# One-hots, selection matrix and centroid parts on 128 rows instead of 120, in a cluster-and-convolve kernel

## The reference

```python
xn = x / jnp.maximum(jnp.linalg.norm(x, axis=1, keepdims=True), EPS)
cn = centroids / jnp.maximum(jnp.linalg.norm(centroids, axis=1, keepdims=True), EPS)
sim = jnp.einsum('bchw,nc->bnhw', xn, cn)
idx = jnp.argmax(sim, axis=1)
onehot = jax.nn.one_hot(idx, N, dtype=x.dtype)                  # N = 40
sum_x = jnp.einsum('bhwn,bchw->bnc', onehot, x)
count = jnp.sum(onehot, axis=(1, 2))
centroids_local = sum_x / jnp.maximum(count, 1.0)[..., None]
gathered = centroids_local[jnp.arange(B)[:, None, None], idx]
delta = jnp.transpose(gathered, (0, 3, 1, 2)) - x
alpha = jnp.exp(-jnp.mean(delta * delta, axis=1, keepdims=True))
y = x + alpha * delta
out = jnp.einsum('oc,bchw->bohw', W, y) + b[None, :, None, None]
return jax.nn.relu(out)
```

## Time and profile before

| | |
|---|---|
| median of the runs | 433.23 us (432.71 to 433.5) |
| profiled execution, its own time | 433.72 us |
| its span, first to last instruction | 431.9 us |
| granted clock of TensorE | 1.000 over the span |
| busy: PE, PEld | 424.5 us (98%), 296.9 us (69%) |
| busy: VectorE, ScalarE, GpSimd | 285.3 us (66%), 243.7 us (56%), 206.8 us (48%) |
| share of PE in the chain that ended last | 95% |

### The profile page before, as it was taken

One profiled execution on the slowest core, in us unless ns is written; L12 is line 12 of the kernel. 1 busy time (PEld: TensorE's weight loads), 2 busy tenths in 40 slices (PEclk: granted clock), 3 DMA queues, 4 the chain that ended last, 5 costly groups with the idle time before them and its releaser, 6 DMA issues.

```text
span 431.9 us, 5788 instructions
## 1 busy us (share of the span) xinstructions
PE 424.5 (98%) x2134; PEld 296.9 (69%) x2134; DVE 285.3 (66%) x377; ACT 243.7 (56%) x329; POOL 206.8 (48%) x102
## 2 busy tenths in 40 slices
PE   8999999999999999999999999999999999999996
PEld 6745466775777667775867757776677758777785
DVE  2458979495775767495873957767674956777730
ACT  5565385566564673564754665656735647555542
POOL 2000565486283582674553862834826745324330
PEclk9999999999999999999999999999999999999999
DMA  8996198976488846859379665878464220222133
GB/s 278 306 289 118 43 250 221 279 217 168 144 232 200 206 186 148 223 142 266 99 194 253 180 160 147 238 193 220 170 152 141 98 99 0 98 99 97 45 112 135
DMA packets 70927, 73.94 MB, mean 171 GB/s; under 512 B 2724, under 2 KB 45732, under 8 KB 70900
## 3 DMA queue, kind: packets, MB, share of 16 engines
q1 hardware_dynamic: 70900, 73.58, 62.0%
HBM read 48.40 MB, written 25.17 MB: 170 GB/s over the span
## 4 chain that ended last, share of the span: by engine, by line
PE 95%; DVE 2%; ACT 1%; issue 1%; POOL 0%; POOLq 0%; DVEq 0%
PE main L793 20%; PE main L795 19%; PE main L794 19%; PE sump L736 10%; PE fa L696 9%; PE gat L767 5%; PE al L774 1%; PE al L815 1%; PE fa L705 1%; PE al L775 1%; PE fa L720 1%; PE main L836 1%; PE al L781 1%; PE gat L781 1%; DVE xt L311 1%; PE gat L808 1%
## 5 line engine op out<-in xcount | busy, mean ns | idle before, releaser
L281 POOL TENSOR_TENSOR z<-z,x 128x1024 f32<-128x1024 f32 x42 | 99.4, 2386 | 148.5 <-DVE z L386 148.5
L793 PE MATMUL main<-yh,wh 128*128 128x512 f32 x376 | 153.1, 407 | 0.0
L795 PE MATMUL main<-yh,wl 128*128 128x512 f32 x376 | 147.1, 391 | 0.0
L794 PE MATMUL main<-yl,wh 128*128 128x512 f32 x376 | 147.0, 391 | 0.0
L288 POOL TENSOR_TENSOR yl<-z,yh 128x1024 fp32r<-128x1024 f32 x44 | 106.1, 2426 | 58.8 <-ACT yh L526 58.8
L366 DVE TENSOR_TENSOR z<-gat,x 128x1024 f32<-128x1024 f32 x46 | 56.2, 1221 | 92.4 <-PE gat L767 92.4
L534 ACT ACTIVATE o<-main,bcol 128x512 f32<-128x512 f32 x96 | 65.9, 687 | 84.5 <-PE main L795 84.4
L793 PEld LDWEIGHTS main<-yh,wh 128*128 128x128 f32 x376 | 70.6, 188 | 20.8 <-issue 4.6
L795 PEld LDWEIGHTS main<-yh,wl 128*128 128x128 f32 x376 | 70.6, 188 | 15.7
L794 PEld LDWEIGHTS main<-yl,wh 128*128 128x128 f32 x376 | 70.7, 188 | 14.5
L526 ACT ACTIVATE yh<-z 128x1024 fp32r<-128x1024 f32 x48 | 50.5, 1052 | 22.9 <-POOL z L281 21.9
(11 more groups left out here) (113 smaller groups left out, 326.9 us busy)
## 6 DMA issues: line engine op xcount, KB each, us to landing
x<-x SPq DMA_DIRECT2D x24, 1024.0 KB, 5.8
out<-o SPq DMA_DIRECT2D x23, 1024.0 KB, 4.9
xs<-x SPq DMA_DIRECT2D x84, 256.0 KB, 6.1
o<-w SPq DMA_DIRECT2D x1, 1024.0 KB, 12.2
out<-o SPq DMA_DIRECT2D x4, 256.0 KB, 2.1
sq<-centroids SPq DMA_DIRECT2D x2, 80.0 KB
bcol<-bias SPq DMA_DIRECT2D x1, 2.0 KB, 11.7
```

Source lines behind the costliest of these rows:

```text
L281: pool.tensor_tensor(z, z, X[g // PARTS % 2][:, pair(h), span(g)], ALU.add).then_inc(y_pool, 1)
L793: t_.matmul(main[:, o % 2, :], WH[:, k, rows], YH[g % 2][:, k, :], start=(k == 0), stop=False)
L794: t_.matmul(main[:, o % 2, :], WH[:, k, rows], YL[g % 2][:, k, :], start=False, stop=False)
L795: last = t_.matmul(main[:, o % 2, :], WL[:, k, rows], YH[g % 2][:, k, :], start=False, stop=(k == KC - 1))
```

## The change

`NK`, the number of columns of `oh3` and `select` and of rows of `ohT`, `part` and `G`, goes from 120 to 128. The last eight columns of `oh3` are set to zero once, at the start on VectorE; those of `select` are zero from the memset on GpSimd that now covers 128 columns. The rows 120 to 127 of `ohT`, `G` and the rest are then computed as zeros. No instruction changes its place in any engine's program; one memset on VectorE is added, and the semaphore `const_done` counts to 8 instead of 7.

```diff
-NK = COPIES * N
+USED = COPIES * N
+
+NK = P
@@
-        oh3 = sb("oh3", [P, PARTS * TILES, COPIES, N], BF16)
+        oh3 = sb("oh3", [P, PARTS * TILES, NK], BF16)
         ohT = [sb(f"oht{j}", [NK, HW], BF16) for j in range(2)]
@@
-        select = sb("select", [P, COPIES, N], F32R)
+        select = sb("select", [P, NK], F32R)
@@
-        select0 = OUT[1][:, 0, 0:NK].rearrange("p (r n) -> p r n", r=COPIES)
+        select0 = OUT[1][:, 0, 0:NK]
+        select_rows = select0[:, 0:USED].rearrange("p (r n) -> p r n", r=COPIES)
@@
-            pool.memset(select0[:, :, :], 0.0).then_inc(ident_done, 1)
+            pool.memset(select0, 0.0).then_inc(ident_done, 1)
@@
-            pool.tensor_copy(select[:, :, :], select0[:, :, :]).then_inc(const_done, 1)
+            pool.tensor_copy(select[:, :], select0).then_inc(const_done, 1)
@@
             v_.memset(oh[:, :, :], 0.0).then_inc(const_done, 1)
+            v_.memset(oh3[:, :, USED:NK], 0.0).then_inc(const_done, 1)
@@
-                a_.activation(oh3[:, :, :, :], oh[:, :, 0:N].unsqueeze(2).to_broadcast(
+                a_.activation(oh3[:, :, 0:USED].rearrange("p s (r n) -> p s r n", r=COPIES), oh[:, :, 0:N].unsqueeze(2).to_broadcast(
                     [P, PARTS * TILES, COPIES, N]), ACT.Copy).then_inc(oh3_done, 1)
@@
-                        last = t_.transpose(dst, oh3[:, slot(u, t), :, :].rearrange("p r n -> p (r n)"), identb[:, :])
+                        last = t_.transpose(dst, oh3[:, slot(u, t), :], identb[:, :])
@@
-                rows = select[:, :, :].rearrange("p r n -> p (r n)")
+                rows = select[:, :]
                 t_.matmul(mean(b), rows, sumsH[:, :], start=True, stop=False)
                 t_.matmul(mean(b), rows, sumsL[:, :], start=False, stop=True).then_inc(cop_done, 1)
```

More of the change, by code:

```diff
@@ L262, in _ @@
                                base=0, pattern=[[-1, P]], channel_multiplier=1).then_inc(ident_done, 1)
-            pool.affine_select(out=select0[:, :, :], in_=select0[:, :, :], compare_op=ALU.not_equal, fill=1.0,
+            pool.affine_select(out=select_rows, in_=select_rows, compare_op=ALU.not_equal, fill=1.0,
                                base=0, pattern=[[0, COPIES], [-1, N]], channel_multiplier=1).then_inc(ident_done, 1)
@@ L425, in _ @@
             v_.reciprocal(s(6), s(5)).then_inc(norm_step, 1)
-            dve.wait_ge(const_done, 7)
+            dve.wait_ge(const_done, 8)
             keep_transposed()
@@ L508, in square @@
                     act.wait_ge(wT_ps, KC)
-                    act.wait_ge(const_done, 7)
+                    act.wait_ge(const_done, 8)
                 elif h == 0:
@@ L850, in _ @@
             transpose_weights(1)
-            pe.wait_ge(const_done, 7)
+            pe.wait_ge(const_done, 8)
             sum_clusters(0, 0)
```

## The result

The change makes the kernel a little faster: 431.33 us (median of 15 runs, 430.95 to 432.24) against 433.14 us for the kernel before (15 runs beside them), a ratio of 0.9964 with a 95% interval of 0.9958 to 0.9971. The medians differ by 1.8 us; the ratio stands for 1.6 us, between 1.3 and 1.8 by its interval. The forecast was no difference.

A forecast was written before the change was run, and what follows sets the result against it. The prediction took TensorE (PE) to bound the kernel. Its terms were all taken as 0, so it forecast the median of the runs before, 433.2 us, no difference (chance 0.84), with a range of 432.3 to 434.2.

The forecast's parts named there:

- the signs: Twelve transposes clearly off 0.83 us, gathers' step reaching 0.23, or a gather's load beginning with the matmul ahead.
- What bounds the kernel: TensorE, busy 424.5 of 431.9 us and 95% of the chain; time changes only where its matmuls follow faster or slower.
- The 96 transposes: One-hots' transposes, 12 per image: loads fall from 133 to about 98 ns, step stays 55 ns; 0 expected.
- the third rival: Faster: the load sets the transposes' step, 3.4 us less, 2.9 for sure, 430.3 us; chance 0.08 with smaller gains.
- The gathers: 96 matmuls with `G` and `ohT` going to 128 rows: step stays 0.22 us; 0 expected, at worst 1.15 us lost.
- the holds: 44 late loads of gathers, 15.8 us idle on PEld; at most about 0.5 us back if full rows end them; 0 taken.
- The second rival: Slower: full rows bring the 96 gathers to the fp32r matmuls' step, 1.15 us more, 434.4 us; chance 0.08.
- The matmuls with `select`: 16 fp32r matmuls: load grows from 181 to 188 ns under a 0.24 us step; 0, at worst 0.1 us.
- ScalarE and VectorE: Same elements on 128 partitions instead of 120, and a gapped copy into `oh3` covered by 6 us; 0 expected.
- The start: GpSimd's `select` memset 7 ns longer, one added VectorE memset, both under existing waits; 0 expected.
- The sum: All terms add to 0, so the earlier median of 433.2 us stays; under 0.87 us counts as no difference.

The follow-up runs named there:

- `wide_transposes`: Kernel before with 128 columns only in `oh3` (moved to the end of SBUF) and the transposes: 0.9985, 416.88 us from 51st to last matmul.
- `pitch_only`: Kernel before with `oh3` at the end of SBUF, tiles 256 bytes apart instead of 240, 120 columns loaded: 0.9987, 416.88 us from 51st to last matmul.
- the aligned layout: `c_t`, `ident`, `identb`, `ones`, `select` allocated right behind `G`: kernel after so edited 0.9945 to before; with 120 rows and columns, 0.9956.
- `narrow_moved`: Kernel before, 120 wide, plus unused bytes so tensors behind `oh3` have the kernel after's addresses: 0.9968, 415.81 us from 51st to last matmul.
- `wide_unmoved`: Kernel after, 128 wide, with `oh3` and `select` at the end of SBUF, other tensors at old addresses: 0.9988 to before, 416.85 us from 51st matmul.

## Why the prediction was wrong

The range was 432.3 to 434.2 and the measured time 431.33. None of the signs came by which the prediction would have known itself wrong: twelve transposes still take 0.83 us, the gathers and their loads are as they were. All of them watched the widened instructions, and the time was lost and won beside these. Step by step:

- *What bounds the kernel.* Right. All that was gained was gained on TensorE, in the steps of its matmuls.
- *The 96 transposes.* Right in what was costed: loads at 98 ns, a step set by the moving side, 0 gained from the load. The saving on PEld was mis-sized: 96 x 35 ns = 3.4 us was announced, the group's busy time fell from 6.5 to 5.9 us and PEld's in all from 296.9 to 296.0, because the loads overlap each other, which the same paragraph had said. `wide_transposes` and `pitch_only` settle the third rival: with loads of 98 or of 133 ns from the same places the time is the same. What the paragraph has nothing on is the matmuls behind the transposes, which get faster or slower with the distance between the tiles.
- *The gathers.* Right: 0, the mean 384 ns, the holds as many and as long with 128 rows as with 120. The second rival (rows make the step of the fp32r matmuls) is refuted: the second gather of a pair follows after the same 226 to 228 ns and the next 128-element or 512-element bf16 work 215 or 216 ns after it, with 120 rows and with 128.
- *The matmuls with `select`.* Their loads grew by 7 ns as expected and cost nothing in the kernel after. That a wider load could be worth something was not among the bounds; in the aligned layout it is 0.3 us, by the steps behind it.
- *ScalarE and VectorE.* As forecast: L561 at 1451 ns, the copy into `oh3` at a median of 1405 ns where it had 1404.
- *The start.* The widths cost nothing there, as forecast. That the start itself differs by over 1 us between executions, by the clock, was missing: the 432.3 to 434.2 had 0.4 us each way for the spread of the runs, taken from three of them, and the 15 runs of before lie between 432.24 and 433.77.
- *The sum.* The step that failed is "The sum is 0", and ahead of it the sentence that the change "adds no instruction to TensorE and moves none", from which I took that only widened instructions could change their time. The term that is missing is the layout: a tensor that grows by 192 bytes moves all the small operands of TensorE, and with them the steps of some 600 matmuls by 2 ns and more each, most of them by 2 to 12, down more often than up. It is worth 1.37 us (`narrow_moved`), the widths and the distance of the `oh3` tiles together 0.07 us more. The rows that would have led there were at hand: the earlier trace rows have 0.24 and 0.23 us where a settled convolution has 0.227, and I used them as the fp32r matmuls' own step, a constant. A look at ten steps in a row would have shown that they decay from 240 to 227 after each interlude, and that the convolution, at a mean of 229.2 ns for some 1000 of these steps, would take some 2 us less at 227: that is room that the sum did not name.

What stays open is the mechanism. Shown is, for `ones`, that the remainder of its address to 256 bytes decides the steps at the pair, that at remainder 128, where the weights and the moving data stand, the step is 227 ns at once, and that two loads from 0, 64 or 192 are felt in it and in up to ten or so matmuls behind them, in values that come in a fixed series. With all weights at remainder 0 and the data at 128 the step never settles. That reads like a rule that a load and the data that move beside it must agree in the remainder, but it is not shown: no run moved the data, so the loads may as well want 128 whatever the data have. Nor is the remainder of the load all there is: at remainder 0 `ones` is followed by 240 235 233 236, `select` with 128 columns (`wide_unmoved`) by 230 231 236 228, and with 120 columns (before) by 232 240 227 231. What the moving operand, the rows and the columns do, why the series is as it is, and why behind gathers, similarities and transposes it remains even with all operands in line, was not tried.

## What to carry to other kernels

Where TensorE is the bound, a change that only grows or shrinks a small buffer is a change of the whole layout behind it: compare it with a kernel that has the old widths at the new addresses before giving the widths credit. Try loaded operands that stand between matmuls of another kind (here `ones` and `select`) at the same remainder to 256 bytes as the weights; it costs an order of allocation, `ones` alone gave 0.35% here, and all small operands in line 0.55% together with the change. (The identities, which are the moving side of the transposes here, gained nothing by it.) And look at the steps of one kind of matmul one by one, not at its mean: a series that decays after each interlude is time that can be had.

## What the runs showed of the hardware

- The step of 128x512 fp32r matmuls on one core was 227 ns when settled and 224 to 241 in and behind the pair with `ones`, when these were loaded from another remainder to 256 bytes than 128; it never settled (mean 232.5 ns) with all weights at remainder 0 and the data at 128.
- A bf16 load of 128 columns takes 98 ns, one of 120 columns 133 ns, with 128 rows as with 120. By the Trainium skill, page "TensorE: Matmul & The Clock Gate", section "Weight-path perf modes — Fast Weight Load (FWL) and DoubleRow", the fast load wants 128 weights of a type that is not fp32; the trace agrees. It bought nothing here: twelve transposes take 0.83 us with either load, and `wide_transposes` and `pitch_only` the same 416.88 us.
- The clock of the first matmuls rose to its full level at 5.73 to 8.76 us into the span, in 15 executions of nearly the same program. Their 51st matmul started at 9.74 to 11.13 us; that difference of 1.4 us is as much as the change is worth. Two profiled executions can't be subtracted from end to end at this scale.
